# Splitting ten of fifteen probability tiles, storing weight halves and redrawing the opening of a fused decoder layer

## What is computed

```python
def reference(x, ctx_4096, ...):
    x = _layernorm(x + _L0_attn_ref(x, Wq, bq, Wk, bk, Wv, bv))
    x = _layernorm(x + _L0_xattn_ref(x, ctx_4096, Wq, Wk, Wv, Wo, q_norm_w, k_norm_w))
    return _layernorm(x + _L0_ffn_ref(x, router_weight, router_bias, expert_bias))
...
    kv = jnp.concatenate([context, latents], axis=1)
    q, k, v = latents @ Wq, kv @ Wk, kv @ Wv      # split in heads of 128
    q, k = rms_norm(q, q_norm_w), rms_norm(k, k_norm_w)
    scores = jnp.einsum('bhgqd,bhkd->bhgqk', qg, k) * scale
    probs = jax.nn.softmax(scores, axis=-1)
    out = jnp.einsum('bhgqk,bhkd->bhgqd', probs, v)
    return out.reshape(bsz, q_len, HEADS * HEAD_DIM) @ Wo
```

## Time and profile before

| | us |
|---|---|
| median of 3 runs | 2921.55 (2919.27 to 2922.64) |
| the profiled execution | 2920.32 |
| its span | 2918.5 |
| TensorE busy | 2791.9 |
| GpSimd busy | 2428.4 |
| VectorE busy | 2164.7 |
| ScalarE busy | 2066.0 |

### The profile page before, as it was taken

How to read it: one execution, slowest core, us unless ns; L and a number is a source line. 1 busy time by engine, 2 the same in 40 slices (tenths; PEclk the granted TensorE clock), 3 DMA queues, 4 the chain that set the end, 5 groups by cost and what they waited for, 6 DMA issues and landing times. The chain is left out here.

```text
span 2918.5 us, 46903 instructions
## 1 busy us (share of the span) xinstructions
PE 2791.9 (96%) x14860; PEld 2228.7 (76%) x14860; DVE 2164.7 (74%) x3483; ACT 2066.0 (71%) x3867; POOL 2428.4 (83%) x2283
## 2 busy tenths in 40 slices
PE   6999999999999999999999999999999999999976
PEld 4767787777777777778888888888888888888744
DVE  4667787777787778777777777777777777777755
ACT  3666777777676777777777777777777777777741
POOL 4488899889888999898888888888888888888880
PEclk9999999999999999999999999999999999999985
DMA  5633443333343434343444434334334333333201
GB/s 194 202 116 116 137 138 127 133 128 120 126 137 131 140 120 139 124 132 127 135 141 141 133 125 151 127 129 131 131 113 140 105 127 113 110 115 105 65 8 69
DMA packets 155604, 364.81 MB, mean 125 GB/s; under 512 B 12761, under 2 KB 48091, under 8 KB 155360
## 3 DMA queue, kind: packets, MB, share of 16 engines
q1 hardware_dynamic: 153608, 359.98, 37.1%
q10 hardware_dynamic: 1752, 1.84, 0.2%
HBM read 323.89 MB, written 37.88 MB: 124 GB/s over the span
## 5 line engine op out<-in xcount | busy, mean ns | idle before, releaser
L707 POOL TENSOR_TENSOR acc<-acc,scores 128x512 f32<-128x512 f32 (+1 forms) x832 | 1110.3, 1334 | 92.0 <-ACT scores L1061 51.8
L1364 DVE SCALAR_TENSOR_TENSOR running_max<-S_ps,rk,running_max 128x512 f32<-128x512 f32 (+1 forms) x896 | 668.8, 746 | 222.7 <-ACT scores L1047 216.6
L689 POOL TENSOR_TENSOR P_lo<-scores,P_hi 128x512 fp32r<-128x512 f32 x512 | 674.6, 1318 | 168.2 <-ACT scores L1061 168.0
L1047 ACT ACTIVATE scores<-S_ps,rk 128x512 f32<-128x512 f32 (+1 forms) x960 | 652.1, 679 | 200.9 <-PE S_ps L774 194.6
L1348 DVE TENSOR_TENSOR scores<-scores,Mb_ps 128x512 f32<-128x512 f32 (+1 forms) x960 | 648.4, 676 | 163.1 <-PE Mb_ps L922 163.1
L1061 ACT ACTIVATE scores<-scores 128x512 f32<-128x512 f32 (+1 forms) x960 | 596.6, 622 | 72.8 <-DVE scores L1348 71.7
L772 PE MATMUL S_ps<-QT_hi,KT_hi 128*128 128x512 f32 (+1 forms) x960 | 552.6, 576 | 27.0 <-DVE running_max L1364 24.0
L1060 ACT ACTIVATE P_hi<-scores 128x512 fp32r<-128x512 f32 x512 | 321.3, 628 | 263.8 <-DVE scores L1348 240.7
L774 PE MATMUL K_ps<-Wkv_hi,kvT 128*128 128x256 f32 (+1 forms) x1664 | 471.4, 283 | 0.0
L772 PE MATMUL K_ps<-Wkv_hi,kvT 128*128 128x256 f32 (+1 forms) x1664 | 470.6, 283 | 0.0
L773 PE MATMUL K_ps<-Wkv_lo,kvT 128*128 128x256 f32 (+1 forms) x1664 | 470.5, 283 | 0.0
(11 more groups left out here) (230 smaller groups left out, 5055.2 us busy)
## 6 DMA issues: line engine op xcount, KB each, us to landing
kvT<-kvT_scratch SPq DMA_DIRECT2D x403, 512.0 KB, 3.3
w_stage<-in_L_xattn_Wq SPq DMA_DIRECT2D x64, 512.0 KB, 4.2
w_stage<-in_L_xattn_Wo SPq DMA_DIRECT2D x64, 512.0 KB, 4.3
kvT_scratch<-built SPq DMA_DIRECT2D x45, 512.0 KB, 3.0
xrow<-in_ctx SPq DMA_DIRECT2D x48, 256.0 KB
w_stage<-in_L_xattn_Wk SPq DMA_DIRECT2D x32, 256.0 KB, 2.9
w_stage<-in_L_xattn_Wv SPq DMA_DIRECT2D x32, 256.0 KB, 3.2
kvT_scratch<-kvT SPq DMA_DIRECT2D x13, 512.0 KB, 3.7
```

Source lines behind the costliest of these rows:

```text
L689: e.tensor_tensor(P_lo[n % 2][0:r, :], prob(t)[0:r, :], f(P_hi[n % 2][0:r, :]), ALU.subtract)\
L707: e.tensor_tensor(a[0:r, :], a[0:r, :], prob(t)[0:r, :], ALU.add).then_inc(s_acc, 1)
L1047: e.activation(row[s % RING][0:r, :], S_ps[s % 2][0:r, :], ACT.Copy, scale=rk[0:r, v % 2, j:j + 1])\
L1364: e.scalar_tensor_tensor(a, src, k, a, ALU.mult, ALU.max).then_inc(s_top, 1)
```

## The change

Four things. (1) `FULL` is now 4, 5, 10, 11 and 14, so ten tiles of a half are split for PV instead of eight; `P_hi` and `P_lo` have three buffers each, and a buffer is waited for three split tiles back. (2) The later self-attention's products stand at tiles 4, 10 and 14, and a quarter is summed three steps after its product instead of one. (3) `split` is done only for the eight units of the first batch; SP stores the two halves (2 x 512 KB) of each chunk to `weight_halves_scratch`, and from unit 8 on `load_halves` loads both from there straight into the operand buffers. (4) The opening starts at step -20: the self projections stand ahead of the step's other jobs, the quarter sums of the first two tiles are spread over steps, and tiles 10 to 14 of unit 0 are projected in steps 0 to 4. On ScalarE `copy_OT` now stands ahead of `exp`.

```diff
-    FIRST = -16
+    FIRST = -20
-    FULL = [2, 3, 6, 7, 10, 11, 14]
+    FULL = [4,5,10,11,14]
+    PB = 3
...
     OPENING = {
-        -16: [("X", 0, 2)],
...
-        -8: [("KV", 0, 5), ("KT", 0, 0), ("X", 0, 0), ("X", 0, 1)],
-        -7: [("Q", 0, 0, 0), ("Q", 0, 0, 1), ("X", 0, 10)],
...
+        -20: [("X", 0, 2)],
...
+        -9: [("X", 0, 0), ("KV", 0, 5)],
+        -8: [("Q", 0, 0, 0), ("Q", 0, 0, 1)],
+        -7: [("X", 0, 1), ("X", 0, 8)],
...
+        -1: [("QT", 0, 0)],
+        0: [("KV", 0, 10), ("X", 0, 14)],
...
     def splits(s):
...
-        return [chunk] if chunk and 0 <= chunk[1] < UNITS else []
+        return [chunk] if chunk and 0 <= chunk[1] < KVH else []
+
+    def reused(s):
+        v, c = divmod(s + AHEAD, CYCLE)
+        chunk = {5: ("Wkv", v + 1, 0), 11: ("Wq", v + 1, 0), 13: ("Wq", v + 1, 1), 14: ("Wo", v - 2, 1),
+                 24: ("Wo", v - 1, 0)}.get(c)
+        return [chunk] if chunk and KVH <= chunk[1] < UNITS else []
...
-        SELF_AT[[-15, -15, -13, -12, -11, -10, -9, -8][t]].append(("turn", t))
-        SELF_AT[[-14, -13, -12, -11, -10, -9, -8, -7][t]].append(("project", t))
-    for t in range(TPB):
-        for k, part in enumerate(("products", "scores", "normalise", "residual", "layernorm")):
-            SELF_AT[-13 + k].append((part, t))
-    EVENTS = [s for s in range(WAIT + 4, LAST) if (s - WAIT) % NJ in (2, 6, 10)]
+        SELF_AT[[-20, -20, -17, -16, -15, -14, -13, -12][t]].append(("turn", t, 0))
+        SELF_AT[[-19, -18, -16, -15, -14, -13, -12, -10][t]].append(("project", t, 0))
+    SELF_AT[-18] += [("products", 0, 0)]
+    SELF_AT[-17] += [("products", 1, 0), ("qk sum", 0, 0), ("qk sum", 1, 0)]
...
+    SELF_AT[-8] += [("rsqrt", 1, 0), ("layernorm", 1, 0)]
+    EVENTS = [s for s in range(WAIT + 4, LAST) if (s - WAIT) % NJ in (4,10,14)]
...
-            LATER[at[i] + 1].append(("qk sum", t, i))
+            LATER[at[i] + 3].append(("qk sum", t, i))
...
-            LATER[at[6 + i] + 1].append(("pv sum", t, i))
+            LATER[at[6 + i] + 3].append(("pv sum", t, i))
...
+            def store_halves(chunk):
+                kind, v, a = chunk
+                e.wait_ge(s_wh, W_AT[chunk] + 1)
+                e.wait_ge(s_wl, W_AT[chunk] + 1)
+                for i, half in enumerate(halves(chunk)):
+                    e.dma_start(whd[v, KINDS.index((kind, a)), :, i, :], f(half)).then_inc(halves_stored(chunk)[0], 16)
+
+            def load_halves(chunk):
+                kind, v, a = chunk
+                if kind == "Wkv":
+                    done = s_wk[v % 2]
+
+                    e.wait_ge(s_kt, NJ * (v - 1))
+                elif kind == "Wq":
+                    done = s_wq
+
+                    e.wait_ge(s_qf, 2 * v)
+                else:
+                    done = s_wo
+
+                    e.wait_ge(s_ff, F_AT["O", 2 * v + a - 1, 1] + 1)
+                e.wait_ge(*halves_stored((kind, v % KVH, a)))
+                for i, half in enumerate(halves(chunk)):
+                    e.dma_start(f(half), whd[v % KVH, KINDS.index((kind, a)), :, i, :]).then_inc(done, 16)
...
-                if n >= 2:
-
-                    e.wait_ge(s_pv, half_tile(n - 2) + 1)
+                if n >= PB:
+
+                    e.wait_ge(s_pv, half_tile(n - PB) + 1)
...
             for s in STEPS:
-                if 0 <= s - WAIT < NS:
-                    exp(s - WAIT)
                 last = s - WAIT - LAG - NJ
                 if last >= 0 and last % NJ == 0 and last // NJ < HALVES:
                     copy_OT(last // NJ)
+                if 0 <= s - WAIT < NS:
+                    exp(s - WAIT)
```

More of the change, by code:

```diff
@@ L201, in attention @@
     W_AT = {x: n for n, x in enumerate(CHUNKS)}
+    REUSED = [x for s in STEPS for x in reused(s)]
+    KINDS = [("Wkv", 0), ("Wq", 0), ("Wq", 1), ("Wo", 0), ("Wo", 1)]
     W_STEP = {x: s for s in STEPS for x in splits(s)}
@@ L278, in attention @@
         row = [ring[:, i, :] for i in range(RING)]
-        P_hi = [sb(f"P_hi{i}", [P, QW], F32R) for i in range(2)]
-        P_lo = [sb(f"P_lo{i}", [P, QW], F32R) for i in range(2)]
+        P_hi = [sb(f"P_hi{i}", [P, QW], F32R) for i in range(PB)]
+        P_lo = [sb(f"P_lo{i}", [P, QW], F32R) for i in range(PB)]
         Wkv_hi = [sb(f"Wkv_hi{i}", [P, C, 2 * HD], F32R) for i in range(2)]
@@ L343, in attention @@
         F_ps = [ps(f"F_ps{i}") for i in range(2)]
-        sa_x = [sem(f"self_rows_loaded{i}") for i in range(2)]
+        sa_x = [sem(f"self_rows_loaded{i}") for i in range(4)]
         sa_qs = [sem(f"self_qkv_stored{i}") for i in range(2)]
@@ L373, in attention @@
         sa_d1 = sem("self_qk_products_of_DVE")
-        sa_sc = sem("self_scores_summed")
+        sa_sc = [sem(f"self_scores_summed{t}") for t in range(TPB)]
         sa_mx = sem("self_row_max")
@@ L382, in attention @@
         sa_d2 = sem("self_pv_products_of_DVE")
-        sa_o = sem("self_outputs_summed")
+        sa_o = [sem(f"self_outputs_summed{t}") for t in range(TPB)]
         sa_h = sem("self_residual_added")
@@ L593, in _ @@
             load_rows(0, TPB)
-            for chunk in CHUNKS[:2]:
-                weights(chunk)
+            weights(CHUNKS[0])
             load_rows(0, TPB + 1)
@@ L598, in _ @@
             load_self(3)
+            weights(CHUNKS[1])
             for s in STEPS:
                 v, c = divmod(s + AHEAD, CYCLE)
-                for part, t in SELF_AT[s - 1]:
+                for part, t, _ in SELF_AT[s - 1]:
                     if part == "layernorm":
@@ L605, in _ @@
                         store_qkv(t)
-                for part, t in SELF_AT[s]:
+                for part, t, _ in SELF_AT[s]:
                     if part == "turn" and TPB <= t < SELF - 2:
@@ L629, in _ @@
                         store_later(t)
-                for n, chunk in enumerate(CHUNKS):
-                    if n >= 2 and W_STEP[CHUNKS[n - 2]] + 2 == s:
-                        weights(chunk)
+                for chunk in splits(s - 2):
+                    n = W_AT[chunk] + 2
+                    if n < len(CHUNKS):
+                        weights(CHUNKS[n])
+                    store_halves(chunk)
+                for chunk in reused(s):
+                    load_halves(chunk)
                 for x in fill(s - 2):
@@ L807, in pv @@
                     ins = three(OT_ps[:], V_hi[v % 2][0:r, i, :], V_lo[v % 2][0:r, i, :],
-                                P_hi[n % 2][0:r, :], P_lo[n % 2][0:r, :], first, last)
+                                P_hi[n % PB][0:r, :], P_lo[n % PB][0:r, :], first, last)
                 ins.then_inc(s_pv, 1)
@@ L952, in _ @@
                     scores(s)
+                for part, t, _ in SELF_AT[s]:
+                    if part == "project":
+                        self_project(t)
+                for part, t, _ in SELF_AT[s]:
+                    if part == "turn":
+                        self_turn(t)
                 for x in fill(s):
@@ L1191, in _ @@
                     copy_OT(last // NJ)
+                if 0 <= s - WAIT < NS:
+                    exp(s - WAIT)
+                for part, t, _ in SELF_AT[s]:
+                    if part == "exp":
+                        self_exp(t)
+                    elif part == "rsqrt":
+                        self_rsqrt(t)
+                for part, t, _ in SELF_AT[s]:
+                    if part == "project":
+                        self_copy_qkv(t)
+                for part, t, _ in SELF_AT[s]:
+                    if part == "turn":
+                        self_copy(t)
                 for kind, v in rooted(s - 2):
@@ L1336, in later, with opening_self @@
                     e.tensor_scalar(b_x[:], b_x[:], mv[:, 0:1], rs[:, 4:5], ALU.subtract, ALU.mult).then_inc(sb_x1, 1)
-            SELF_STAGE = {"products": self_products, "scores": self_scores, "normalise": self_normalise,
-                          "residual": self_residual, "layernorm": self_layernorm}
+            def opening_self(part, t, i):
+                if part == "products":
+                    self_products(t)
+                elif part == "qk sum":
+                    self_qk_sum(t, i)
+                elif part == "max":
+                    self_max(t)
+                elif part == "normalise":
+                    self_normalise(t)
+                elif part == "pv sum":
+                    self_pv_sum(t, i)
+                elif part == "residual":
+                    self_residual(t)
+                elif part == "layernorm":
+                    self_layernorm(t)
             def shift(t):
@@ L1456, in _ @@
             for s in STEPS:
-                for part, t in SELF_AT[s]:
-                    if part in SELF_STAGE:
-                        SELF_STAGE[part](t)
+                for part, t, i in SELF_AT[s]:
+                    opening_self(part, t, i)
                 if 0 <= s - WAIT < NS:
```

128 lines of the change are left out of this document (87 added, 41 removed), and 20 rows, old and new, of the table OPENING.

## The result

The changed kernel takes 2868.82 us (median of 4 runs, 2867.32 to 2870.06), 0.982 of the kernel before (95% interval 0.9803 to 0.9837). The forecast was 2848 in a range of 2815 to 2888: the sign and the range hold, the middle was 21 us too low. Two terms of the sum failed outright, and one was right by errors that cancel.

A forecast was written before the change was run, and what follows sets the result against it. TensorE was taken as the bound, with 61 us of stall in units 1 to 13 entering through VectorE's order. Terms -11, -14.7, -37.9, -11.9 and +2.5 gave -73, so 2848 us with the median's 1.2; range 2815 to 2888.

The forecast's parts named there:

- Opening and unit 0: Start of kernel: 10 us for the first scores and 1 more for unit 0's waits, -11 (bounds -20 and +3).
- a sign that I had named: Opening: the forecast counts as wrong if the first scores start after 88 us.
- Units 1 to 5: GpSimd at 83.3 and TensorE at 83.0 are level; 85.0 us per unit taken (bounds 83.3 and 88), -14.7.
- The first rival: Units 1 to 5: GpSimd becomes the bound, units stay at 88 to 89, +18, total 2866; chance 15%.
- Units 6 to 13: VectorE's waits go, ten tiles save 0.7 a unit, 1.0 us of stall stays in each: -37.9.
- worth nothing by itself: Stored weight halves: GpSimd gets 7 us lighter per unit in most of the run, where it bounds nothing.
- Units 14 to 30: Four more split tiles a unit at 0.17 us each on TensorE, -0.7 per unit, -11.9 in all.
- The end: Tail after the last units, set by GpSimd: +2.5 us together.
- my two terms: Tail: GpSimd's added low parts less weight subtractions, +0.5; last output projection waiting for a load of halves, +2.
- an argument against a rival: Units 1 to 5: three-deep P buffers, cited against GpSimd becoming the bound (+18, 15%).
- VectorE's own work: VectorE's stall is its added work on later tiles, not the wait: half of 61 us stays, +27, 2875; 15%.
- key tiles behind the halves: SP's queue: halves block key tiles, TensorE waits in each of 24 units, +120, 2968; chance 6%.

The follow-up runs named there:

- The sums alone: Kernel before, with only the later quarter sums changed (products at tiles 4, 10 and 14, sums three steps after): 2873.1 us, ratio 0.9844.
- eight split: Changed kernel with the full-precision tiles of before, so eight split tiles a half instead of ten, three buffers kept: 2853.2 us, ratio 0.9777.
- two heads' weights: Changed kernel with only the weights of heads 0 and 1 split and stored, all later units loading those halves: 2839.3 us, a single run.
- the sums and three buffers: Kernel before with the later sums and three buffers of high and low parts, eight split tiles, every weight split in every unit: 2873.7 us.
- the rows earlier: Changed kernel with the next batch's rows asked for six steps ahead of their transposes instead of four: 2868.2 us.

## Why the prediction was right or wrong

**Opening and unit 0: wrong, -11 against +6.6.** The step was "there are some 10 us of idle to win". The idle was won and spent: TensorE is busy 48.7 of the first 60 us instead of 39.9, the six later tiles' projections among it, and then 5.0 us less than before from 60 to 86, at a lower clock. Of the 6.1 us by which the first projection came earlier, 5.2 were left at the queries' projection and 1.25 at the first scores. I summed the idle time of an engine instead of following the chain to the first scores, which runs through VectorE's drains; that they start after 88 us was a sign that I had named. Unit 0 I priced at -1. The sums alone make it 4.1 shorter, yet it took 7.2 more, so the rest of the change costs 11 there: a wait of 3.4 us for a late context row, four more low parts and a mean clock of 0.91, among them. An estimate of the share of the clock, 0.09 of 76.6 us, is at most some 7 of these.

**Units 1 to 5: wrong, -14.7 against +0.1.** The step was "the two are level ... I take 85.0", between GpSimd's 83.3 and TensorE's 83.0. GpSimd's work came as forecast, 413.1/5 = 82.6, but the unit took 88.0. Over the kernels here GpSimd at 78.3 us of work gives 85.0 (eight split), at 72 gives 83.7 (two heads' weights). So GpSimd, in order and with uneven work before a queue two steps deep, binds here at 94% busy; that the unevenness is the reason is argued and not shown. The first rival was what happened; I gave it 15%. That its 2866 also met the total is luck: these units (+15) and the opening (+18) missed upwards, the late units (-8) and the end (-2) downwards. That the sums were worth 13.6 us here is shown by the kernel with the sums alone; ten tiles took them back.

**Units 6 to 13: right by luck, with three terms off.** The sums alone give -27.7 where I had -32.3 (1.0 us of stall left in each unit). The halves, "worth nothing by itself", give 13.1 more (682.1 with the sums and three buffers, 669.0 with the halves too), and ten tiles cost 2.7 instead of gaining 5.6.

**Units 14 to 30: the mechanism right, the size short.** Four tiles at 0.17 us gave 0.7; the eight-tile kernel shows 0.67 in units 23 to 30 and 0.72 in units 15 to 22, 11.1 us in all for the 11.9 of the sum. The other 0.45 us, 7.8 in all, had no term. It is a wait of TensorE for one low part behind a split, in a stretch that I had called "TensorE's own work" because its busy time was 99.8% of the window. An estimate by the Trainium skill's page "FP8 and Floating Point Precision" (TensorE Precision Notes), which has true FP32 as four passes, would have given 0.9 for the passes; the trace's 0.17 per tile was the right one to take. The 1.10 and 0.93 us of the earlier trace rows both hold the first pass of the next scores, 0.23 us, as well; without it a full tile takes 0.87 and a split one 0.70, and their difference is the same.

**The end: +2.5 against +0.7.** GpSimd does set it, and the last output projection does wait 4.6 us for its `Wo_lo` (before 3.7 for `OT_lo`), but my two terms were small parts of larger ones: two more split tiles a half cost 4.3 there (191.6 against 187.3) and the rest of the change gives 3.4 back against the sums with three buffers (190.7).

**What the sum had no term for: the third buffer.** I used it as an argument against a rival and never asked what ten tiles would do without it: 140 us. And the halves with ten tiles are worth 82 us over the whole kernel (2951.1 against 2868.8), not nothing. The parts don't add: with eight tiles, halves and new opening together are worth 20.5 (2873.7 to 2853.2). The rivals on VectorE's own work and on key tiles behind the halves did not come: waits of VectorE on later products fell to 1.9 us, and TensorE's waits in the changed kernel hold none for a key tile's transfer, though halves land in 5.5 and 6.4 us; with the rows earlier there is one, of 2.4 us.

## What to carry to other kernels

Price a part of a change in the company of the others: ten split tiles were worth -0.7 us a unit in the late units, where GpSimd had lost its splits, nothing in units 8 to 13, where the later self-attention tiles still ran, +1.8 to +2.9 where the splits were still there, and +4.6 more with one buffer less. When two in-order engines feed each other at nearly equal work per unit, don't take the larger of the two as the time; here a helper at 94% busy cost over 4 us in 88, and at 86% little. Choose such a parameter per stage, by what else the helper engine does there, down to the last units, where its backlog is the end of the kernel. And where a change shortens idle time, follow the chain to the first thing that is wanted before booking the gain.

## What was not expected of the hardware

Units 23 to 30 of the kernel before, with TensorE counted busy 660.7 of 662.2 us, still held a delay of 0.44 us each: the modelled ends of matmuls cover most of it (the records show 0.19). It shows as a distance between starts (0.79 against 0.35 us in the rows above). A wait of 3 us can cost more than itself, but need not: behind the late row four transposes take 1.11 us, the clock being at the lower of its two levels (0.50 granted), and behind a wait of 3.19 us for the same row in the eight-tile kernel they take 0.66, at full clock. The same subtraction of 128x1024 took 1.37 us on VectorE and 2.39 to 2.41 on GpSimd.
